# Flamingo-style two-layer block on one core: context split and key bound of the second layer made in the first expert layer, its norms in the attention block, first queries in the output banks

## The reference

```python
x = x + tanh(g_xattn[0]) * L0_xattn(ctx, layernorm(x), mask)   # keys and queries normalised per head
x = x + tanh(g_ffn[0])   * L0_ffn(layernorm(x))                # 8 experts of 512, top 2, relu
x = x + tanh(g_xattn[1]) * L1_xattn(layernorm(x), ctx)         # one null key and value, no mask
x = x + tanh(g_ffn[1])   * L1_ffn(layernorm(x))                # 8 experts of 64, top 2, gelu

def L1_xattn(x, context):
    x = stable_layernorm(x, g_in)      # divides by the row's maximum, then normalises
    q = (x @ Wq) * 64 ** -0.5
    k, v = split(context @ Wkv)        # the raw context: layer 1 does not normalise it
    # null key and value in front, softmax over the keys, times v, then Wo
    return stable_layernorm(out @ Wo, g_out)
```

## Time and profile before

| | |
|---|---|
| median of 3 runs | 4353.86 us (4353.84 to 4357.28) |
| the profiled execution | 4354.57 us |
| its span, first to last instruction | 4352.7 us |
| PE busy over the span | 4034.8 us (93%) |
| DVE / ACT busy | 3388.4 us (78%) / 3161.1 us (73%) |
| POOL busy | 419.9 us (10%) |
| mean granted TensorE clock | 0.976 |

### The profile page before, as it was taken

The page is one execution under the profiler, slowest core; times in us unless marked ns, Lnnn a source line. Parts: engine busy times, 40 slices in busy tenths (PEclk is TensorE's granted clock), DMA queues, the critical chain, the costliest instruction groups (busy, mean ns, idle before and its releaser), DMA issues. The chain is left out here.

```text
span 4352.7 us, 65636 instructions
## 1 busy us (share of the span) xinstructions
PE 4034.8 (93%) x25721; PEld 2650.6 (61%) x26161; DVE 3388.4 (78%) x5202; ACT 3161.1 (73%) x5110; POOL 419.9 (10%) x339
## 2 busy tenths in 40 slices
PE   3999999999999999999977599999999999999995
PEld 2666666666666666666656366666666666666663
DVE  5788788787888888888767577777777787777775
ACT  3888888888988888888843367676766666666662
POOL 3111111111111121111100000000000000000000
PEclk9999999999999999999988699999999999999997
DMA  1000000000000000000012000000000000000001
GB/s 40 1 1 16 1 5 12 1 16 1 16 1 1 16 1 16 1 1 18 1 43 82 4 1 16 1 16 1 5 12 5 13 1 16 1 16 1 15 1 43
DMA packets 29159, 50.25 MB, mean 12 GB/s; under 512 B 9118, under 2 KB 17574, under 8 KB 26790
## 3 DMA queue, kind: packets, MB, share of 16 engines
q1 hardware_dynamic: 26788, 45.33, 3.3%
q10 hardware_dynamic: 2066, 0.69, 0.1%
HBM read 45.15 MB, written 0.85 MB: 11 GB/s over the span
## 5 line engine op out<-in xcount | busy, mean ns | idle before, releaser
L835 DVE TENSOR_TENSOR a_probs_lo<-a_probs 128x1024 fp32r<-128x1024 f32 x1760 | 2124.7, 1221 | 564.3 <-ACT a_probs L675 255.9
L671 ACT ACTIVATE a_probs<-scores_ps,a_c_bias,a_k_rstd 128x512 f32<-128x512 f32 x1888 | 1312.1, 775 | 31.0 <-PE scores_ps L1156 30.6
L1181 PE MATMUL out_ps<-a_probs_lo,a_v 128*128 128x512 f32 x3520 | 1134.6, 443 | 0.0
L675 ACT ACTIVATE a_probs<-scores_ps,a_c_bias 128x1024 f32<-128x1024 f32 x816 | 867.7, 1112 | 115.8 <-PE scores_ps L1156 115.5
L1174 PE MATMUL out_ps<-a_probs,a_v 128*128 128x512 bf16 x3080 | 848.8, 389 | 84.9 <-issue 59.0
L1156 PE MATMUL scores_ps<-a_q_hi,a_k_hi 64*128 64x512 f32 x3520 | 790.3, 444 | 8.0 <-ACT a_probs L671 7.7
L1181 PEld LDWEIGHTS out_ps<-a_probs_lo,a_v 128*128 128x128 f32 x3520 | 658.2, 188 | 218.7
L1156 PE MATMUL scores_ps<-a_q_lo,a_k_hi 64*128 64x512 f32 x3520 | 700.0, 392 | 0.0
L1156 PE MATMUL scores_ps<-a_q_hi,a_k_lo 64*128 64x512 f32 x3520 | 695.7, 390 | 0.0
L1174 PEld LDWEIGHTS out_ps<-a_probs,a_v 128*128 128x128 f16 x3520 | 272.5, 97 | 560.1 <-issue 303.0
L640 ACT ACTIVATE a_v<-proj_ps 128x256 f16<-128x256 f32 x448 | 172.3, 384 | 488.1 <-PE proj_ps L1091 488.0
(11 more groups left out here) (233 smaller groups left out, 3317.6 us busy)
## 6 DMA issues: line engine op xcount, KB each, us to landing
a_den<-a_inv_row SPq DMA_DIRECT2D x16, 1024.0 KB, 4.7
normed<-in_L_xattn_we_g SPq DMA_DIRECT2D x16, 256.0 KB, 2.7
m_gate_spread<-m_combine_row SPq DMA_DIRECT2D x8, 512.0 KB, 3.9
a_wkv_raw<-in_L_xattn_wkv_g SPq DMA_DIRECT2D x16, 128.0 KB, 2.1
a_wo_raw<-in_L_xattn_wo_g SPq DMA_DIRECT2D x16, 128.0 KB, 2.0
m_w_raw<-in_L_ffn_w1T SPq DMA_DIRECT2D x8, 256.0 KB, 4.3
m_w_raw<-in_L_ffn_w2T SPq DMA_DIRECT2D x8, 256.0 KB, 4.5
m_gate_spread<-m_combine_row SPq DMA_DIRECT2D x8, 256.0 KB, 5.3
```

The costliest lines, as they stand in the source:

```text
L671: ins = nc.scalar.activation(probs[:, pb, e * 512:(e + 1) * 512], scores[:, b, e * 512:(e + 1) * 512], ACT.Exp, bias=cbias[:, tile:tile + ...
L675: ins = nc.scalar.activation(probs[:, pb, :], scores[:, b, :], ACT.Exp, bias=cbias[:, 1:2] if last else cbias[:, 0:1])
L835: nc.vector.tensor_tensor(plow[:, idx % NPL, :], probs[:, idx % NB, :], p_hi[:, idx % NB], ALU.subtract).then_inc(plo_ready, 1)
L1181: nc.tensor.matmul(outs[:, e * 512:(e + 1) * 512], v32[:, c % 2, t, e, :], plow[:, idx % NPL, e * 512:(e + 1) * 512], start=False, stop=t ...
```

## The change

It does these things:

- **Layer 0's preparation** keeps the mean and variance of each context row (`cms`), by one copy more on DVE.
- **The expert layer 0** gets new work. SP loads `w_k` right behind the gate's weights, and the context rows again (`ctx_rows`, 50 tiles and the rest) behind the first two experts' weights and ahead of the gates' rows. PE makes the 16 Gram matrices before it transposes the normed rows, now into `out_ps`. From step k = 3 on, after every second `project(k)`, PE transposes four context tiles into `proj_ps` (13 parts, `turn_ctx`), ACT copies their high part one step later and DVE their low part another step later. The key bound is made at k = 3 (DVE, from `cms` and the squared Gram matrices), on POOL, and at k = 15 (DVE).
- **Layer 1 has no preparation block.** Its attention block starts at once. SP's first DMAs there are the first key, value and query weights; ACT issues the six small loads and then splits the weights; DVE norms the queries' rows itself, with the low parts of the first weights and of item 0 in between; PE projects item 0 and 1 before it transposes the normed rows, then projects the queries.
- **First queries in the output banks** (both layers): group 0's `project_q` and `transpose_q` write the two halves of `out_ps` (`q_ps`) instead of `proj_ps`, so the second half waits for no reader, and the items in `proj_ps` wait for no query.
- **Both attention heads**: POOL no longer fills `out_acc` (L596), and ACT splits the first weights before it waits for the constants.

The diff, cut to its core:

```diff
@@ flamingo @@
+        cms = sb("ctx_moments", [P, CTX_FULL + 1, 2])
...
+            attention_layer(nc, A, 0, sem, sb, layer_norm, ln_stats, ln_apply, rstd, shared)
+            shared["ctx_hi"] = sb("a1_x_hi", [P, (CTX_FULL + 1) * P], R32, keep)
+            shared["ctx_lo"] = sb("a1_x_lo", [P, (CTX_FULL + 1) * P], R32, keep)
+            shared["kbound2"] = sb("a1_key_bound2", [P, H + GH], F32, keep)
+            moe_layer(nc, A, 0, sem, sb, layer_norm, rstd, out, shared)
+            attention_layer(nc, A, 1, sem, sb, layer_norm, ln_stats, ln_apply, rstd, shared)
+        moe_layer(nc, A, 1, sem, sb, layer_norm, rstd, out, shared)
@@ attention_layer, preparation: only for L == 0 now @@
+                        step(nc.vector.tensor_copy(B["cms"][:, :, :], part[:, :, 6:8]))
@@ attention_layer, attention block @@
+        def q_ps(r, b):
+            return outs[:, b * 512:(b + 1) * 512] if r == 0 else proj[:, :]
...
-                step(nc.gpsimd.memset(oacc[:, :, :], 1.0))
...
+                if L == 1:
+                    rstd(pool, QT, var_ready, rstd_ready, 1)
+                    first(nc.gpsimd.memset(lift[0:DH, :], 1.0))
+                    first(nc.gpsimd.memset(lift[DH:P, :], 1.0 / LIFT))
+                    rstd(pool, QT, var_ready, rstd_ready, 2)
+                    pool.wait_ge(tr_done, len(jobs))
+                    first(nc.gpsimd.memset(Y[:, :, :], 0.0))
...
-                act.wait_ge(consts, NCONST)
+                if L == 1:
+                    for dst, name in (...six small loads...):
+                        act.dma_start(dst, name).then_inc(w_in, 16)
                 wkv_split(0)
                 wq_split(0)
+                act.wait_ge(consts, NCONST)
...
+                else:
+                    read_kv(0, 0)
+                    k_high(0, 0)
+                    v_wide(0, 0)
+                    read_kv(0, 1)
+                    act.wait_ge(w_in, 16 * 6)
+                    for i, job in enumerate(jobs):
+                        hi, lo, w = job_out(*job)
+                        act.wait_ge(tr_done, i + 1)
+                        nc.scalar.activation(hi, scores[:, 0, i * 512:(i + 1) * 512], ACT.Copy, scale=col[:, 0:1]).then_inc(xh_done, 1)
+                    k_high(0, 1)
+                    v_wide(0, 1)
+                    for b in range(2):
+                        q_rows(0, b)
+                    q_square(0)
+                    read_kv(0, 2)
...
+                    lstep = Steps(dve, ln_step)
+                    ln_stats(dve, lstep, X, 0, QT, B["few"], var_ready)
+                    constants()
+                    wkv_low(0)
+                    wq_low(0)
+                    ln_apply(dve, lstep, X, Y, 0, QT, B["few"], rstd_ready, 1)
...                    row maximum, reciprocal, product
+                    ln_stats(dve, lstep, Y, 0, QT, B["few"], var_ready)
+                    v_low(0, 0)
+                    k_low(0, 0)
+                    ln_apply(dve, lstep, Y, Y, 0, QT, B["few"], rstd_ready, 2)
+                    dve.sem_inc(lat_ready, 1)
+                    v_low(0, 1)
...                    low parts of the normed rows, k_low(0, 1), null key and value
                     bound_norm(0)
                     null_rows(0)
                     bound_null(0)
+                    v_low(0, 2)
...
+                else:
+                    project_kv(0, 0, 0, None)
+                    transpose_k(0, 0)
+                    project_kv(0, 1, 0, None)
+                    for i, (kind, tiles, at) in enumerate(jobs):
+                        pe.wait_ge(lat_ready, 1)
+                        for j, t in enumerate(tiles):
+                            last = nc.tensor.transpose(scores[:, 0, (4 * i + j) * P:(4 * i + j + 1) * P], Y[:, t, :], ident[:, :])
+                        last.then_inc(tr_done, 1)
+                    transpose_k(0, 1)
+                    for b in range(2):
+                        pe.wait_ge(tr_read, b + 1)
+                        project_q(0, b, None)
+                    project_kv(0, 2, 0, None)
+                    for b in range(2):
+                        transpose_q(0, b, None)
+                    transpose_k(0, 2)
@@ moe_layer, L == 0 @@
+            PARTS = [list(range(i, min(i + 4, CTX_FULL + 1))) for i in range(0, CTX_FULL + 1, 4)]
+            TURN0 = 3
+            def part_at(k):
+                i = (k - TURN0) // 2
+                return i if k >= TURN0 and (k - TURN0) % 2 == 0 and i < len(PARTS) else None
...  SP
+                    sp.dma_start(w_k[:, :], A["L1_xattn_Wkv"][:, 0:H * DH]).then_inc(wk_in, 16)
                     weights(0)
                     weights(1)
+                    sp.dma_start(raw[:, 0:CTX_FULL, :], ...).then_inc(ctx_in, 16)
+                    sp.wait_ge(zeroed, 1)
+                    sp.dma_start(raw[0:CTX_REST, CTX_FULL, :], ...).then_inc(ctx_in, 16)
                     save_combine(sp)
...  ACT, after the splits of step k
+                        i = part_at(k - 1)
+                        if i is not None:
+                            at, w = part_cols(i)
+                            act.wait_ge(ctx_turned, i + 1)
+                            nc.scalar.activation(ctx_hi[:, at], proj[:, 0:w], ACT.Copy).then_inc(ctx_hi_done, 1)
...  DVE, after hidden_low(k)
+                        i = part_at(k - 2)
+                        if i is not None:
+                            dve.wait_ge(ctx_hi_done, i + 1)
+                            nc.vector.tensor_tensor(ctx_lo[:, at], proj[:, 0:w], ctx_hi[:, at].bitcast(F32),
+                                                    ALU.subtract).then_inc(ctx_lo_done, 1)
+                        if k == 3:
...                            two products and a maximum over cms; sum of wsq (128x51 and 64x1024)
+                        if k == 15:
+                            dve.wait_ge(bnd_out, 3)
...  PE
+                    pe.wait_ge(wk_in, 16)
+                    for h in range(H):
+                        ...Gram matrix of head h into outs...
+                    last.then_inc(gram_done, 1)
                     pe.wait_ge(z_ready, ONCE)
...
+                    def turn_ctx(i):
+                        if i:
+                            pe.wait_ge(ctx_lo_done, i)
+                        else:
+                            pe.wait_ge(ctx_in, 32)
+                            pe.wait_ge(ct_read, ONCE)
+                        for j, t in enumerate(PARTS[i]):
+                            last = nc.tensor.transpose(proj[:, j * P:(j + 1) * P], raw[:, t, :], ident[:, :])
+                        last.then_inc(ctx_turned, 1)
...
                         project(k)
+                        i = part_at(k)
+                        if i is not None:
+                            turn_ctx(i)
```

308 lines of the change are left out of this document (154 added, 154 removed).

## The result

The kernel after the change takes 4304.31 us (median of 4 runs, 4303.47 to 4306.81), the kernel before 4354.72 us beside it (4 runs): ratio 0.9884, 95% interval 0.9867 to 0.9901, 50.4 us less. The forecast was 4304.1 in a range of 4296 to 4314. The profiled execution took 4306.81 us with a span of 4304.9, 47.8 us less than the span of before.

A forecast was written before the change was run, and what follows sets the result against it. Bounds: layer 1's fully exposed preparation chain, then layer 1's head and POOL's bound in layer 0. Terms -2.5 + 8.3 - 55.6 = -49.8 from 4354.57 gave 4304.8, median 4304.1 us; range 4296 to 4314.

The forecast's parts named there:

- Layer 0, -2.5: Layer 0's head: ACT's splits start earlier (-1.5 us) and queries' second half stops waiting for ACT's copy (0.95); range -1.5 to -2.6.
- (a): Expert layer: PE makes the Gram matrices first, delaying the chain through router and first hidden layer; +1.3 us (0.5 to 1.7).
- (b): Expert layer's loop: 51 context transposes on PE add in full, 0.55 us for four; 7.0 us (6.0 to 9.4).
- (c): Expert layer's loop: ACT's copies and DVE's differences stay hidden; 0, up to 4 us if semaphores take up the slack.
- (d): Expert layer, SP's queue: the context's load ahead of the gates' rows is hidden, landing by 2276.6 at the latest; 0.
- Expert layer, +8.3: First expert layer: sum of its added work in Gram matrices, transposes, copies and loads; +8.3 us (+6.5 to +15).
- Layer 1, -57.0: Layer 1, block start to first exponential: 45.3 us in place of 102.3, with POOL ending last; -57.0 us.
- The clock after the idle time, +1.4: Layer 1's loop start: it starts after an idle PE, as in layer 0; +1.4 us (0.9 to 2.5).
- Not hidden: Rival, expert loop: PE, ACT and DVE take turns on one PSUM bank, 17.5 us for 7.0; 4314.6; chance 0.14 including SP's queue.
- Head spared more: Rival, layer 1's head: POOL's 6.0 us before its reduction is paid once, in the expert layer; 4298.1; chance 0.10.
- Clock falls in the loop: Rival, expert loop: the 51 transposes pull the clock down, up to 71 us more; 4375; chance 0.02.
- Slow issues: Rival, layer 1's head: ACT's sixth issue still takes 2.74 us, making the rest 2.2 us later; 4306.3; chance 0.13.

## Why the prediction was right, point by point

**Layer 0, -2.5: measured -2.75.** The two parts (banks 0.95, constants 1.5) measured 0.94 and 1.44; the other 0.37 came from POOL's answer, which the prediction had held fixed. The term that failed is the 0 for the rest of layer 0: 1.62 us were lost between the first exponential and the expert block, 1.2 of it in the loop's groups. The prediction priced the copy of the moments (0) and not the place of the buffer; of the 1.2, the widened buffer gave 0.8 back in one trace and all in another.

**(a) Gram matrices, +1.3.** They started at 2253.39 and ended near 2257.0; rows, router and all behind them began 1.5 us later relative to the block, inside the 0.5 to 1.7. But nothing of it is left at the stage's end: without them the stage took 116.8 us, with them 115.6 to 116.8, because they bring the clock up for a while 8 to 11 us sooner, and for good up to 3 us sooner. The prediction had this as half of a rival (the clock rises up to 6 us earlier and spares up to 3) and should have had it in the sum, with the bounds of that rival.

**(b) Turns, +7.0.** Without Gram matrices the stage is 6.66 us longer than before, which is the turns and all that goes with them. The estimate of 0.55 for four was right within 0.03 by that, which is closer than the stage's spread of about 1 us lets one tell. Four transposes took 0.60 from start to end, and 0.36 to the next matmul.

**(c) Copies, 0, (d) SP, 0.** PE had 0.1 us idle in 86. The last turn ended before 2349.5. "Lands by 2276.6 at the latest" holds: the DMA engines were idle from 2268 on. The late load shows what a miss costs: 14.7 us.

**Expert layer, +8.3: +6.05.** 2.2 too much; the nine traces with the same instructions in this stage give +5.5 to +6.7, so it was too much in all of them. 0.3 of it lies in (b), the rest in (a), where 1.3 us stood for work that cost nothing in the end.

**Layer 1, -57.0: -57.15.** Each mark of the chain fell near the forecast, counted from the block's start: rows at PE 16.1 (16.7), square end 26.0 (26.3), null bound 30.3 (30.6), second score tile done 36.9 (37), POOL's root 43.8 (43.9), exponential 45.1 (45.3). The rows came 0.6 early, at what the prediction had added for the splits in DVE's queue; the queries took 0.3 more. Four of ACT's six issues took 1.02 and 1.13 us in pairs, the others 0.35 and 0.46: no 2.74, that rival falls. The chain's numbers held because each came from a row of the same operation in the kernel before. One part is luck: the queries ran at the lower clock both in the row taken and in the profiled execution. In the four traces where they ran at the full clock, with the same instructions, the square was done 2.1 to 2.5 us sooner, which the prediction did not foresee.

**The clock after the idle time, +1.4: +1.74,** and the run with work behind the score tiles shows it to be the clock.

**What nobody forecast.** The last expert layer took 43.7 us in place of 41.4 with the same instructions; the clock rose later in it. In other kernels of this study it took 41.9 to 43.9. The median lies 2.5 us under the profiled execution, where the prediction took 0.7.

**The rivals.** Not hidden: refuted by PE's 0.1 us idle. Head spared more: POOL paid its 6.0 us anew in layer 1, as the prediction had argued from the row. But it was right that these 6 us can be spared, and wrong about how; not an earlier call but an earlier place in the queue does it. Clock falls in the loop: refuted, even at four times the turns. Slow issues: refuted.

**The range.** The lower bound of the sum, -60, does not follow from the terms: -2.6, +6.5 and -57 add to -53.1. The range of 4296 to 4314 was set by the rivals and does not rest on it.

That the total was hit within 0.2 us is luck; that it fell well inside the range is not. The profiled execution came out 2.0 us above the 4304.8 forecast for it: the expert layer was 2.2 cheaper and the two heads 0.4, against layer 0's loop with 1.6, the last expert layer with 2.3 and layer 1 behind its first exponential with 0.7 dearer. The median then lay 1.8 us further under the profiled execution than assumed.

## What to carry to other kernels

Work that hangs on no result of the stage can go into a neighbouring stage that one engine fills; its price there is its own time on that engine (here 6.7 us for 51 transposes), and its gain is the whole chain that it formed where it stood (57 us in layer 1, of which the moments save 14.3 without any move), provided its load is issued early enough that no queue holds it. Look behind the word "issue" in a row: a step of the engine's own can sometimes be put ahead of the wait (6 us in a head, by removing one increment that nobody waits for). Before reordering a queue, ask which buffer the moved instruction sets free.

## What the runs showed of the hardware

- In the heads a partition reduction on POOL starts 5.7 to 6.5 us after its input, or after the operation ahead of it, when its configuration step (MODIFY_POOL_CONFIG in the trace) is issued only then, and 0.1 to 0.3 us after it when that step has run during the wait.
- Matmuls whose results nobody reads can speed a head up: 8 of them (3.4 us at the lower clock) ahead of layer 0's queries halved the step between these, from 0.21 to 0.11 us, and 3.68 us of Gram matrices at the lower clock did not lengthen their stage (116.8 us without them in one run, 115.6 to 116.8 with them).
- 204 transposes among some 350 other matmuls of a loop left the clock at 1.00. In layer 1's head, in the run with 24 unused matmuls, it fell behind two idle stretches of 0.9 and 1.1 us, and the 10 us of work that followed ran at the lower level.
- Moving all later buffers by 408 bytes a partition made layer 1's loop 0.9 us in 1585.6 slower, the same in eleven traces, and layer 0's 0.6 to 1.2 in 1849.0; with 512 bytes, in two traces, 0.6 and 0.7 us of layer 1's came back.
- In layer 0's head the row of the granted clock shows 1.00 in some traces and 0.50 in others while the same matmuls take the same 0.41 us: ahead of the first change of the clock in a trace the column isn't to be trusted, the durations are.
